# A decoder's first attention: tiles in pairs, weighting behind the keys, a later exponential, and a mask in row halves

## What is computed

```python
x = layernorm(x)
q = einsum('bpd,hde->bphe', x, W_Q) + b_Q          # k, v in the same way
scores = where(causal, einsum('bqhe,bkhe->bhqk', q, k) / sqrt(128), -1e5)
z = einsum('bkhe,bhqk->bqhe', v, softmax(scores))
x = x + einsum('bqhe,hed->bqd', z, W_O) + b_O      # residual
```

## Time and profile before

| | us |
|---|---|
| median of 3 runs | 1754.83 |
| lowest and highest | 1753.07, 1756.31 |
| the profiled execution | 1752.43 |
| its span in the trace | 1750.6 |

### The profile page before, as it was taken

How to read it: one execution, slowest core, us unless ns; L and a number is a source line. 1 busy time by engine, 2 the same in 40 slices (tenths; PEclk the granted TensorE clock), 3 DMA queues, 4 the chain that set the end, 5 groups by cost and what they waited for, 6 DMA issues and landing times. The chain is left out here.

```text
span 1750.6 us, 37012 instructions
## 1 busy us (share of the span) xinstructions
PE 1584.9 (91%) x14664; PEld 1281.7 (73%) x14664; DVE 1089.3 (62%) x1734; ACT 863.5 (49%) x1466; POOL 672.5 (38%) x527
## 2 busy tenths in 40 slices
PE   6999999999996887899999797899997898999998
PEld 4888888888885565777788564566664675888887
DVE  5777677677776888566442568999994565112111
ACT  3555555555453565555422346667672674222222
POOL 0111211211212663531422265999994430232332
PEclk9999999999998999899999799999998898999999
DMA  3011111111112300010102120000000900000000
GB/s 105 16 64 55 40 63 60 33 63 60 37 59 78 109 2 26 8 12 10 40 1 105 28 64 1 1 2 1 2 1 26 360 17 1 1 13 12 1 12 12
DMA packets 72351, 70.26 MB, mean 40 GB/s; under 512 B 24816, under 2 KB 64368, under 8 KB 71840
## 3 DMA queue, kind: packets, MB, share of 16 engines
q1 hardware_dynamic: 72224, 68.46, 12.2%
HBM read 46.03 MB, written 19.27 MB: 37 GB/s over the span
## 5 line engine op out<-in xcount | busy, mean ns | idle before, releaser
L665 POOL TENSOR_TENSOR s_w_parts<-s_w_raw,s_w_parts 128x768 fp32r<-128x768 f32 x15 | 27.8, 1855 | 401.9 <-ACT s_w_parts L615 401.9
L1488 DVE TENSOR_TENSOR s6f_hid<-s6f_act_sb,s6f_u_ps 128x512 f32<-128x512 f32 x64 | 44.0, 688 | 218.4 <-PE s6f_u_ps L1439 218.4
L1511 POOL TENSOR_TENSOR s6f_hid_parts<-s6f_hid,s6f_hid_parts 128x512 fp32r<-128x512 f32 x64 | 82.7, 1291 | 224.3 <-ACT s6f_hid_parts L1477 224.3
L2228 POOL TENSOR_TENSOR s4b_with_q<-s4b_with_q 128x1024 f32<-128x1024 f32 x64 | 150.8, 2378 | 0.4 <-DVE s4b_with_q L2183 0.4
L2183 DVE TENSOR_TENSOR s4b_with_q<-s4b_c_ps,s_q_rows 128x2048 f32<-128x2048 f32 x64 | 146.1, 2285 | 1.2 <-PE s4b_c_ps L2322 1.1
L598 PE MATMUL s_o_ps<-s_w_parts,s_zT 128*128 128x256 f32 x768 | 110.6, 294 | 4.1 <-DVE x_rows L701 4.1
L539 PE MATMUL s_v_ps<-s_wv_parts,s_xnT 128*128 128x256 f32 x768 | 104.6, 286 | 8.2 <-ACT s_v L644 6.8
L1477 ACT ACTIVATE s6f_hid_parts<-s6f_hid 128x512 fp32r<-128x512 f32 x64 | 40.5, 632 | 144.5 <-PE s6f_o_ps L1459 141.0
L539 PEld LDWEIGHTS s_v_ps<-s_wv_parts,s_xnT 128*128 128x128 f32 x768 | 97.0, 191 | 13.8 <-ACT s_v L644 10.0
L1459 PEld LDWEIGHTS s6f_o_ps<-s6w_parts,s6f_hid_parts 128*128 128x128 f32 x768 | 99.2, 188 | 6.8 <-issue 1.0
L598 PEld LDWEIGHTS s_o_ps<-s_w_parts,s_zT 128*128 128x128 f32 x768 | 97.3, 193 | 8.8 <-issue 4.5
(11 more groups left out here) (333 smaller groups left out, 3982.0 us busy)
## 6 DMA issues: line engine op xcount, KB each, us to landing
stored_weights<-s1q_halves SPq DMA_DIRECT2D x16, 768.0 KB, 3.7
s6w_parts<-stored_weights SPq DMA_DIRECT2D x32, 384.0 KB, 7.6
s1q_packed<-in_codes SPq DMA_DIRECT2D x8, 384.0 KB, 4.4
s1q_scale<-in_scale_rows SPq DMA_DIRECT2D x8, 384.0 KB, 4.9
s3p_raw<-in_ffn_pieces SPq DMA_DIRECT2D x8, 384.0 KB, 8.5
early_values<-s_vbd SPq DMA_DIRECT2D x1, 2176.0 KB, 12.3
s_vbd<-early_values SPq DMA_DIRECT2D x4, 544.0 KB, 7.0
x_rows<-in_x SPq DMA_DIRECT2D x4, 512.0 KB, 5.4
```

What stands on the lines that cost most here:

```text
L1488: nc.vector.tensor_tensor(hid[:, f % 2, :], act_sb[:, f % 2, :], u_ps[:, f % 2, :], ALU.mult) \
L1511: nc.gpsimd.tensor_tensor(hid_parts[:, f % 2, 1, :], hid[:, f % 2, :], hid_parts[:, f % 2, 0, :], ALU.subtract).then_inc(low_done, 1)
L2228: nc.gpsimd.tensor_tensor(with_q[:, half, :, 0, :, n_, :], with_q[:, half, :, 0, :, n_, :], with_q[:, half, :, 1, :, 1 - n_, :], op).then_ ...
```

## The change

**Order and lags.** TensorE's step was project 3, turn 4, scores 3, output 5, weigh 4; it is queries 3, turn 5, keys 3, weigh 5, second values 3, output 6, scores 3. The exponential and `normalise` go from lag 3 to 4, the copy of the transposed probabilities and both parts of z from 4 to 5, `add_out` from 5 to 6. `split_high` (lag 0) and `load` stay as they are. GpSimd does the Dequantiser's low part and its sum ahead of `split_low`, where it did them behind it.

**Tiles in pairs.** The tokens of two tiles are interleaved, so that the probabilities of one sequence of each stand beside each other without zeros: per unit two transposes in place of four, `prob` and `probT` of half the width, and one division on VectorE over 128 rows in place of two over 64. `weigh` takes eight matmuls over 64 rows and 64 columns in place of four over 128 rows and 128 columns, into two banks of PSUM. Scores and transposed probabilities share a bank now, with waits of `turn` for `masked` and of `scores` for `pT_out` in return; `prob` and `zT` are doubled.

**Mask in row halves.** Each of the four mask matmuls of `attention16` runs over 64 rows in place of 128, in turn over the lower and the upper ones.

The core of the diff:

```diff
         def rows(t):
+            if pairs:
+                return turned[:, t % 4, 0:D].rearrange("p (c b s) -> p c b s", c=NC, b=2)
             return turned[:, t % 4, 0:D].rearrange("p (c q) -> p c q", c=NC)
+
+        def place(part, t):
+            return parts[:, part, :, t // 2, :, t % 2, :] if pairs else parts[:, part, :, t, :]
 
         @block.vector
...
-        xnT = oroom.sb("xnT", [P, 2, NC, NT, P], F32R)
+        xnT = oroom.sb("xnT", [P, 2, NC, NT // 2, 2, 2, S], F32R)
...
-            v = room.sb("v", [P, G, TG, 2, E])
+            v = room.sb("v", [P, G, 2, 2, 2, E])
             sc = room.sb("sc", [P, TG, S])
             ex = room.sb("ex", [P, TG, S])
             mx = room.sb("mx", [P, TG])
             sm = room.sb("sm", [P, TG])
             rs = room.sb("rs", [P, TG])
-            prob = room.sb("prob", [P, TG, P])
-            probT = room.sb("probT", [P, TG * P])
-            zT = room.sb("zT", [P, 2, TG * P], F32R)
+            prob = room.sb("prob", [P, 2, TG, S])
+            probT = room.sb("probT", [P, TG * S])
+            zT = room.sb("zT", [P, 2, 2, 2, 2 * P], F32R)
             q_ps = room.ps("q_ps", [P, 512])
             k_ps = room.ps("k_ps", [P, 512])
             v_ps = room.ps("v_ps", [P, 512])
-            s_ps = room.ps("s_ps", [P, 512])
-            pT_ps = room.ps("pT_ps", [P, 512])
-            z_ps = room.ps("z_ps", [P, 512])
+            sp_ps = room.ps("sp_ps", [P, 512])
+            s_ps, pT_ps = sp_ps[:, 0:TG * S], sp_ps[:, TG * S:2 * TG * S]
+            z_ps = room.ps("z_ps", [P, 2, 512])
             o_ps = room.ps("o_ps", [P, 2, 512])
...
+                    project(u, k, 0, q_ps, q_full, q_out)
+
+                def project_k(u, rnd, k):
+                    project(u, k, 1, k_ps, k_full, k_out)
+
+                def second_values(u, rnd, k):
+                    if k // G == 0:
+                        values(u, k % G, 1)
+
...
                 def scores(u, rnd, k):
                     pe.wait_ge(q_out, u + 1)
                     pe.wait_ge(k_out, u + 1)
                     wait(pe, masked, u)
+                    wait(pe, pT_out, u - 1)
                     for t in range(TG):
                         for b in range(2):
-                            at = t * P + b * S
+                            at = t // 2 * 2 * P + b * P + t % 2 * S
                             last = nc.tensor.matmul(s_ps[b * S:(b + 1) * S, t * S:(t + 1) * S], qT[:, at:at + S],
                                                     kT[:, at:at + S], start=True, stop=True)
                     last.then_inc(s_full, 1)
@@ -576,8 +591,12 @@
                 def turn(u, rnd, k):
                     pe.wait_ge(prob_done, u + 1)
                     wait(pe, pT_out, u)
-                    for t in range(TG):
-                        last = nc.tensor.transpose(pT_ps[:, t * P:(t + 1) * P], prob[:, t, :], core.c("ident"))
+
+                    pe.wait_ge(masked, min(u + 2, U) if isinstance(u, int) else u + 2)
+                    for pair in range(2):
+                        last = nc.tensor.transpose(pT_ps[:, pair * P:(pair + 1) * P],
+                                                   prob[:, k % 2, 2 * pair:2 * pair + 2, :].rearrange("p t s -> p (t s)"),
+                                                   core.c("ident"))
                     last.then_inc(pT_full, 1)
...
                     pe.wait_ge(v_out, u + k % G + (2 if k < G else -2))
                     wait(pe, z_low, u)
-                    for t in range(TG):
-                        last = nc.tensor.matmul(z_ps[:, t * P:(t + 1) * P], v[:, k % G, t, k // G, :],
-                                                probT[:, t * P:(t + 1) * P], start=True, stop=True)
+                    for pair in range(2):
+                        for b in range(2):
+                            for n in range(2):
+                                rows, at = slice(n * S, (n + 1) * S), pair * P + b * S
+                                last = nc.tensor.matmul(z_ps[:, n, at:at + S], v[rows, k % G, pair, b, k // G, :],
+                                                        probT[rows, at:at + S], start=True, stop=True)
                     last.then_inc(z_full, 1)
...
-                run_steps(pe, U, [(project, 3), (turn, 4), (scores, 3), (output, 5), (weigh, 4)], unroll=8)
+                run_steps(pe, U, [(project_q, 3), (turn, 5), (project_k, 3), (weigh, 5), (second_values, 3), (output, 6),
+                                  (scores, 3)], unroll=8)
...
-                    wait(act, o_full, u)
-                    nc.scalar.activation(zT[:, 0, :], z_ps[:, :], ACT.Identity, bias=bias[:, k // G, 2:3]) \
+                    wait(act, o_full, u - 1)
+                    nc.scalar.activation(zT[:, k % 2, 0, :, :], z_ps[:, :, 0:2 * P], ACT.Identity, bias=bias[:, k // G, 2:3]) \
                         .then_inc(z_high, 1)
 
-                run_steps(act, U, [(v_copy(0), 3), (q_copy, 3), (k_copy, 3), (v_copy(1), 3), (probT_copy, 4), (exponent, 3),
-                                   (z_high_part, 4), (split_high, 0), (deq.scalar, 4)], unroll=8)
+                run_steps(act, U, [(v_copy(0), 3), (q_copy, 3), (exponent, 4), (probT_copy, 5), (k_copy, 3),
+                                   (z_high_part, 5), (v_copy(1), 3), (split_high, 0), (deq.scalar, 4)], unroll=8)
...
-                run_steps(pool, H, [(split_low, 0), (lambda j, rnd, slot: deq.gpsimd_sum(j), 1),
-                                    (lambda j, rnd, slot: deq.gpsimd_low(j, slot), 2)])
+                run_steps(pool, H, [(lambda j, rnd, slot: deq.gpsimd_low(j, slot), 2),
+                                    (lambda j, rnd, slot: deq.gpsimd_sum(j), 1), (split_low, 0)])
...
-                nc.vector.memset(prob[:, :, :], 0.0).then_inc(zeroed, 1)
-                dve.wait_ge(zeroed, 1)
...
-                    for b in range(2):
-                        rows = slice(b * S, (b + 1) * S)
-                        last = nc.vector.tensor_tensor(prob[rows, :, b * S:(b + 1) * S], ex[rows, :, :],
-                                                       rs[rows, :].unsqueeze(2).to_broadcast([S, TG, S]), ALU.mult)
-                    last.then_inc(prob_done, 1)
-
-                run_steps(dve, U, [(shift, 3), (normalise, 3), (z_low_part, 4), (add_out, 5), (deq.vector, 3)],
+                    wait(dve, pT_full, u - 1)
+                    nc.vector.tensor_tensor(prob[:, k % 2, :, :], ex[:, :, :],
+                                            rs[:, :].unsqueeze(2).to_broadcast([P, TG, S]), ALU.mult) \
+                        .then_inc(prob_done, 1)
+
+                run_steps(dve, U, [(normalise, 4), (z_low_part, 5), (shift, 3), (add_out, 6), (deq.vector, 3)],
...
-            nc.vector.tensor_copy(ident_r[:, :], core.c("ident")).then_inc(masks, 1)
+            for b in range(2):
+                rows = slice(b * S, (b + 1) * S)
+                last = nc.vector.tensor_copy(ident_r[rows, :].rearrange("p (a s) -> p a s", a=2),
+                                             core.c("ident")[rows, rows].unsqueeze(1).to_broadcast([S, 2, S]))
+            last.then_inc(masks, 1)
...
-                    nc.tensor.matmul(s_ps[:, j, 0:4 * S].rearrange("p (h s) -> p h s", s=S), ident_r[:, :],
-                                     mask_r[:, :].unsqueeze(1).to_broadcast([P, 4, S]), start=True, stop=False)
+                    half = slice(j % 2 * S, (j % 2 + 1) * S)
+                    nc.tensor.matmul(s_ps[:, j, 0:4 * S].rearrange("p (h s) -> p h s", s=S), ident_r[half, :],
+                                     mask_r[half, :].unsqueeze(1).to_broadcast([S, 4, S]), start=True, stop=False)
```

More of the change, by code:

```diff
@@ L272, with split_tokens @@
 PARTS = ((0, 0), (0, 1), (1, 0))
-def split_tokens(core, parts, mv, factor, tag, column_step=1, beside=None, high_beside=None):
+def split_tokens(core, parts, mv, factor, tag, column_step=1, beside=None, high_beside=None, pairs=False):
     nc = core.nc
@@ L296, in low @@
                 dve.wait_ge(high_done, t + 1)
-                nc.vector.tensor_tensor(parts[:, 1, :, t, :], rows(t), parts[:, 0, :, t, :], ALU.subtract) \
+                nc.vector.tensor_tensor(place(1, t), rows(t), place(0, t), ALU.subtract) \
                     .then_inc(low_done, 1)
@@ L319, in _ @@
                 act.wait_ge(turned_done, t + 1)
-                nc.scalar.activation(parts[:, 0, :, t, :], rows(t), ACT.Copy).then_inc(high_done, 1)
+                nc.scalar.activation(place(0, t), rows(t), ACT.Copy).then_inc(high_done, 1)
                 if high_beside and t in (3, 9):
@@ L481, in low_weights @@
                                     ALU.subtract).then_inc(wv_low, 1)
-        split_tokens(core, xnT, mv, rstd, "s1t", beside=low_weights, high_beside=high_weights)
+        split_tokens(core, xnT, mv, rstd, "s1t", pairs=True, beside=low_weights, high_beside=high_weights)
         with ExitStack() as ctx:
@@ L535, in values @@
                     for n in range(2):
```

(31 more changed lines are left out.)

13 lines of the change are left out of this document (7 added, 6 removed).

## The result

| | us |
|---|---|
| before, median (1753.07 to 1756.31) | 1754.62 |
| changed kernel, median of 4 (1786.53 to 1798.32) | 1793.63 |
| ratio, 95% interval | 1.0219, 1.0183 to 1.0254 |
| the profiled execution, its span | 1798.32, 1796.5 |

The changed kernel is 2.2% slower (1.8 to 2.5%), by 39 us. The page gives the first sight of it: TensorE is busy for 32 us more, at a lower granted clock. The last row is that clock in 40 slices of the span, in tenths of 2.4 GHz; stage 1 lies in the first 13 and a half.

The account below looks back on a forecast made before the run. TensorE was taken as the bound in stage 1. From 1754.8 us, -15.1 + 1.6 - 6.8 - 7 + 42 + 8.4 = +23.1 gave 1778 us, range 1724 to 1800.

Parts of the forecast that it names:

- The load: Stage 1: late weights stop TensorE ahead of weigh, seven even heads 3.9 us each, seven odd 2.1; +42 us.
- The clock: TensorE at 1.2 GHz for about 3 us after each of the seven 3.9 us stops; +8.4 us, bounds 0 and 20.
- Weighting 1.03: Stage 1 weigh: two row groups side by side, eight 128-column loads each; 1.03 us, 0.22 more than now.
- rivals 2 and 3: Weighting: 2, halved by streaming, 0.61 us, total 1751, chance 0.10; 3, groups load in turn, 1.89 us, total 1833, 0.06.
- Units on TensorE: Stage 1: units without values 6.80 to 6.38 us, -15.1 in all; with values +0.05 each, +1.6 in all.
- The values' wait: Stage 1: TensorE's idle time ahead of the values goes, as their second half comes behind keys and weigh; -6.8 us.
- GpSimd's sum: Earlier sum on GpSimd frees VectorE sooner, but nothing on TensorE waits for it; 0 us.
- The mask: Stage 3: mask in two row groups takes 0.39 us a tile for 0.67, over 32 tiles; -7 us, between 0 and -9.0.
- All but stops and clock: Whole kernel without the terms of 42 and 8.4: 1754.8 - 27.3 = 1727.5 us.
- rival 1: The load isn't late where it matters, landing within 2.1 us behind output's end; 1727.5 us, chance 0.15.
- Rival 4: SyncE's store of 768 KB right behind the weights delays their landing by 1.5 us; +21, 1799 us, chance 0.09.

Follow-up runs that it names:

- e1: Changed kernel with a head's weights asked for first and its bias last, so only the bias waits for output: 1731.98 us, ratio to before 0.9867.
- e4: Kernel before, order untouched, with the load of a head's weights waiting for one unit more of output: 1797.26 us, ratio 1.0252.
- e9: Kernel before with a head's weights asked for first and its bias last: 1753.98 us, ratio 0.9997.
- e5: Changed kernel with four (even heads) or two (odd heads) fp32 matmuls, results overwritten, filling the stops ahead of the weighting: 1772.84 us, ratio 1.0104.
- e7: Kernel before with new order and lags, weights first, early sum and new mask, but no pairs of tiles: 1735.50 us, ratio 0.9900.
- e6: e1 with GpSimd's three parts back in the order of before (split_low, sum, low part): 1740.39 us, ratio 0.9918.
- e10: Kernel before with GpSimd's sum and low part ahead of split_low, nothing else: 1743.50 us, ratio 0.9940.
- e12: e1 once more, unaltered, on the same chip as e11: 1729.59 us, ratio 0.9862.
- e11: Kernel before with GpSimd's early sum and the mask in row halves alone: 1737.20 us, ratio 0.9903.

## Why the prediction was right, and where its terms were off

The time, 1793.63, lies in the range (1724 to 1800) and on the side that had a chance of 0.70. It lies 16 us above the forecast of 1778. The movement was +39 against +23.

- **The load, +42.** Right in kind, place, count and order, shown by e1, e4 and e9. The stops measure 36.7 us, 3.5 us on the mean for even heads and 1.7 for odd ones, for 3.9 and 2.1. At the load followed above two inputs were a little high: W_O lands in 2.3 us in place of 2.4, and ScalarE's copies run closer together than with 0.1 of overlap (queries at 303.08, the probabilities' copy at 303.96, its end at 304.33: 1.25 us for 1.33).
- **The clock, +8.4.** This is the step that failed: about +26, by e5. I had expected half clock after the longer stops only, and for about 3 us, from one place at the end of the stage. It came after five of the seven short stops too, and lasted 6.8 us with each of the long ones. The bound of 20 was passed.
- **Weighting 1.03.** Measured 1.04. The construction from neighbours, with eight loads of 128 columns in each of two row groups, holds; rivals 2 and 3 (0.61 and 1.89) are out. In the same place of the step the weighting over 128 rows takes 0.89 (e7), so that the price of the row halves is 0.15, and not 0.22. The loads over 64 rows and 128 columns take 188 ns at the median, those over 128 rows and 128 columns took 192. The Trainium skill's sentence in "TensorE: Matmul & The Clock Gate", section "LDWEIGHTS (loading the stationary operand)", that a load goes by its columns, agrees with this trace. The speedup of up to 2x that the Trainium skill has in "TensorEngine Tiling (Array Packing)", section "Theoretical Speedup", does not show in this shape, while the mask, with 256 moving columns to a load, fell from 0.67 to 0.43.
- **Units on TensorE.** 6.46 for 6.38: turn and keys 1.70 for 1.74, but `output` 1.62 for 1.53, which I had carried over from behind the scores. The units with values: 9.21 (by the timeline from 246.64 to 255.86 scores to scores, 9.22), for 9.16 + 0.05.
- **The values' wait, -6.8.** The amount went, and the new place of the second values is enough for it: with the late sum in the new order (e6), TensorE is idle for 0.1 us ahead of the values' matmuls. But e10 removes the same wait in the old order, with GpSimd's order alone. Either is enough; I had seen only one, and not what the wait came from.
- **GpSimd's sum, 0.** Failed: worth 11 us on the kernel before (e10; the 6.8 above are part of them) and 8.4 on the new order (e6, against e1). "Nothing on TensorE waits for it" was read from direct waits. The chain goes through VectorE's queue, then ScalarE's. And the new wait for `masked`, costed at nothing, isn't nothing when VectorE is late (e6); the early sum hides it.
- **The mask, -7.** Measured 8.
- **All but stops and clock.** I had 1727.5 us (rival 1's figure); e1 has 1732.0 and e12 1729.6. That this comes so close is in part luck. I had 13.5 us for order and pairs, 6.8 for the values' wait and nothing for the sum, 20.3 in all. By e10, e11 and e12 the sum brings 11 with the values' wait in it, and order and pairs 7.6. Units without values got 0.34 us shorter, for 0.42.
- **The rivals.** Rival 1 itself is out: at the two loads followed above ScalarE gets its weights 4.0 and 4.5 us behind output's end, not within 2.1. Rival 4 is out as well: the store goes out at 300.88, right behind the weights, and W_O lands in 2.3 us (DMA issues of after, 230 to 320 us):

```profile
s_w_raw<-in_L_attn_W_O SPq DMA_DIRECT2D x2, 128.0 KB, 2.3
```

## What to carry to other kernels

When a lag in a software pipeline changes, look for everything that waits for the moved part with a lag of its own: here a prefetch that nobody edited went from a step early to a step late, and outweighed everything that the new order won. A wait for several things in one queue should hold only the one that needs it; moving the bias behind the weights was worth 3.4%. And an idle engine's releaser in a profile is only the last link: GpSimd's sum cost 11 us, 6.8 of them through two other queues, and only a run of that part alone showed it.

## What the runs showed of the hardware beyond that

TensorE's clock was less forgiving than expected: in a stream that is busy otherwise, a stop of 1.83 us went with 3.4 us at 1.2 GHz, and one of 3.28 us with 6.8, where an fp32 filling of the same length kept it at 2.4 GHz (e5). VectorE's addition of 128x768 out of SBUF took 2.37 us on the mean in before, where GpSimd ran beside it, and 1.32 in e10, where it does so less. Four transposes of 128x128 take 0.53 us, 0.13 each. Two of them between projections start the next one only 0.14 us later, but they cost more than that: it then takes 1.56 us until the weighting, where a projection behind another one took 1.38.
